# Four attention layers on one core: the third layer's scaling and turning one slot each behind the step before

## What is computed

```python
x = L0(x)   # group norm; q, k, v = h @ w + b (128 wide); softmax(q k / sqrt(C)) @ v + h, over all 256 positions
x = L1(x)   # q, k 16 wide with relu; softmax within a row of 16 positions; gamma * out + x
x = L2(x)   # q, k 16 wide; softmax over all 256 positions; gamma * ctx + x
x = L3(x)   # 8 heads; keys and values from the 3x3 / stride 2 average pool of x; projection w_o, + x

# L2, the third layer, is the one that is changed
q = x @ Wb; k = x @ Wc; v = x @ Wd
attn = softmax(einsum('bnk,bmk->bnm', q, k), axis=-1)
return gamma * einsum('bnm,bmd->bnd', attn, v) + x
```

## Time and profile before

| | before |
|---|---|
| median of the runs | 136.36 us |
| the profiled execution | 136.52 us |
| its span, first to last instruction | 134.6 us |
| granted TensorE clock, mean | 0.975 |
| TensorE busy | 123.1 us (91%) |
| VectorE, ScalarE, GpSimd busy | 83.7, 76.7, 73.2 us |
| third layer, from the first scores to the last output matmul | 55.4 to 80.3 us |

### The profile page before, as it was taken

The page is one execution under the profiler, slowest core; times in us unless marked ns, Lnnn a source line. Parts: engine busy times, 40 slices in busy tenths (PEclk is TensorE's granted clock), DMA queues, the critical chain, the costliest instruction groups (busy, mean ns, idle before and its releaser), DMA issues.

```text
span 134.6 us, 3603 instructions
## 1 busy us (share of the span) xinstructions
PE 123.1 (91%) x1386; PEld 89.6 (67%) x1386; DVE 83.7 (62%) x196; ACT 76.7 (57%) x228; POOL 73.2 (54%) x120
## 2 busy tenths in 40 slices
PE   6887999989999999999899993999949999999990
PEld 4665799977876777667678871423323775988990
DVE  5776666445324564679779430779699999940081
ACT  0436347788985657576987551333425567597320
POOL 8942616999892123320068888504166666799300
PEclk9999999999999999999999999599995999999999
DMA  3950000000000000000000033424455620000046
GB/s 92 328 172 0 0 5 2 2 0 2 0 5 0 5 0 0 5 0 0 0 0 0 27 102 85 140 83 136 63 70 144 83 22 5 5 0 5 5 124 188
DMA packets 19104, 6.41 MB, mean 48 GB/s; under 512 B 9360, under 2 KB 18960, under 8 KB 19088
## 3 DMA queue, kind: packets, MB, share of 16 engines
q1 hardware_dynamic: 17456, 4.93, 15.5%
q10 hardware_dynamic: 1632, 1.27, 3.2%
HBM read 4.61 MB, written 1.57 MB: 46 GB/s over the span
## 4 chain that ended last, share of the span: by engine, by line
PE 73%; DVE 10%; issue 5%; DMA 4%; POOL 3%; ACT 2%; ACTq 0%; DVEq 0%; POOLq 0%
PE bank L749 11%; PE bank L792 9%; PE bank L694 8%; PE bank L771 8%; PE bank L780 5%; PE bank L713 5%; PE bank L733 5%; DMA x_all<-in_x_dram 4%; PE bank L746 3%; PE bank L685 3%; PE bank L809 3%; PE bank L723 2%; PE bank L760 2%; DVE prob L589 2%; DVE negmax L587 2%
## 5 line engine op out<-in xcount | busy, mean ns | idle before, releaser
L416 ACT ACTIVATE prob<-bank,negmax 128x256 f32<-128x256 f32 (+1 forms) x48 | 19.4, 410 | 14.8 <-DVE negmax L549 10.1
L355 POOL TENSOR_TENSOR prob<-prob,inv 128x512 f32<-128x512 f32 x16 | 16.4, 1044 | 16.0 <-DVE inv L599 16.0
L467 ACT ACTIVATE prob<-prob 128x512 f32<-128x512 f32 x16 | 10.1, 630 | 19.9 <-DVE prob L589 19.9
L771 PE MATMUL bank<-kdiag,qT 128*32 128x512 f32 x128 | 17.4, 666 | 2.2 <-issue 2.2
L749 PE MATMUL bank<-probT,v 128*128 128x256 f32 x64 | 17.1, 389 | 0.7 <-issue 0.7
L694 PE MATMUL bank<-packed,xT 128*128 128x128 f32 (+1 forms) x96 | 15.6, 286 | 0.2 <-ACT prob L416 0.2
L577 DVE SCALAR_TENSOR_TENSOR xT<-bank,packed,xT 128x256 f32<-128x256 f32 x16 | 7.7, 482 | 11.7 <-PE bank L749 6.9
L694 PEld LDWEIGHTS bank<-packed,xT 128*128 128x128 f32 x96 | 13.1, 191 | 1.9 <-issue 1.2
L749 PEld LDWEIGHTS bank<-probT,v 128*128 128x128 f32 x64 | 11.1, 190 | 4.1 <-issue 3.1
L792 PEld LDWEIGHTS bank<-probT,vdiag 128*32 128x32 f32 x512 | 11.7, 113 | 3.0 <-issue 3.0
L587 DVE TENSOR_REDUCE negmax<-bank 128x8 f32<-128x512 f32 x16 | 10.6, 663 | 3.6 <-PE bank L771 3.6
(11 more groups left out here) (102 smaller groups left out, 244.5 us busy)
## 6 DMA issues: line engine op xcount, KB each, us to landing
kdiag<-k_rows SPq DMA_DIRECT2D x32, 64.0 KB, 2.5
out_dram<-x_all SPq DMA_DIRECT2D x8, 128.0 KB, 2.0
x_all<-in_x_dram SPq DMA_DIRECT2D x2, 256.0 KB, 4.1
x_all<-in_x_dram ACTq DMA_DIRECT2D x2, 256.0 KB, 5.5
vdiag<-v_rows SPq DMA_DIRECT2D x8, 64.0 KB, 3.2
packed<-in_pack_dram ACTq DMA_DIRECT2D x1, 321.0 KB, 5.8
k_rows<-kT SPq DMA_DIRECT2D x4, 64.0 KB, 2.1
v_rows<-vt SPq DMA_DIRECT2D x4, 64.0 KB, 2.0
```

What stands on the lines that cost most here:

```text
L355: nc.gpsimd.tensor_tensor(p, p, inv[g][:, t, :].unsqueeze(2).broadcast_to([128, HEADS, KEYS]), ALU.mult)\
L416: last = nc.scalar.activation(prob[g][:, t, 0:keys], psum("scores", layer, g)[:, keys * t:keys * t + keys], ACT.Exp, bias=negmax[g][:, t, ...
L467: nc.scalar.activation(prob[g][:, t, :], prob[g][:, t, :], ACT.Exp).then_inc(s_exp3, 1)
L771: last = mm(ps[STRIP * s:STRIP * s + STRIP, :].rearrange("p (c m k) -> p c k m", c=HEADS, m=HKEY), qT[g][:, 0, HTOK * j:HTOK * j + HTOK], ...
```

## The change

The distances of two steps of the third layer become 1 instead of 2: scaling comes one slot behind the scores (and their exponentials), turning one slot behind the scaling. As the distances add up, all later steps start two slots sooner against scores, values and projections, and the list has two slots less.

```diff
-        steps += [("qk", 2, 1), ("v", 2, 1), ("scores", 2, 3), ("scale", 2, 2), ("probT", 2, 2), ("o", 2, 2)]
+        steps += [("qk", 2, 1), ("v", 2, 1), ("scores", 2, 3), ("scale", 2, 1), ("probT", 2, 1), ("o", 2, 2)]
```

## The result

The changed kernel takes 139.74 us (median of three runs, 138.94 to 139.94) against 136.36 us: a ratio of 1.026, with a 95% interval of 1.022 to 1.030. It is slower by 3.4 us. The profiled execution took 138.94 us with a span of 137.0 us, 2.4 us more than before. Executions with a low clock that took over 1.5% longer than the shortest of the same kernel, such as the profiled one of e1 (150.15 us), are left out of every ratio.

A forecast was written before the change was run, and what follows sets the result against it. Bound by the path from ScalarE's first keys copy (kT) through two DMA round trips to the fourth layer's scores. kT +3.8 us, longer idle +0.1: 136.52 + 3.9 = 140.4, median 0.16 lower, 140.3 us; range 138.3 to 142.1.

The forecast's parts named there:

- The ring: Third layer: VectorE's scaling g waits for ScalarE's exponentials g, ahead of maxima g+1; 2.58 us per image against 2.12.
- The two rivals that needed it to be absent: Third layer: shorter pipeline wins, 135.4 us, 6%; TensorE as most-contended engine sets the pace, 136.4 us, 5%.
- The walk: Third layer followed image by image, from maxima 0 at 56.60 to kT at 77.8, 78.2 with the shared resource.
- The bank's tie: Third layer: a pair of scores waits for banks until the previous odd image's exponentials end; +0.32 us for images 2 and 4.
- The shared resource: Third layer: VectorE's scalings 3 to 6 meet GpSimd's pooling inside the ring; 0 to 0.92 us, 0.45 taken.
- From kT to the scores: First keys' copy through two DMA round trips to the fourth layer's first scores: an unchanged 8.12 us.
- The idle time ahead of the scores: TensorE, done with the third layer at 83.6 to 84.0, idles 2.7 to 3 us before the fourth layer's scores.
- The clock: TensorE's 1.2 GHz stretches: one more or less worth up to about 1.5 us; none taken, +0.1 for longer idle.
- the clock falls once more: Rival: another low clock in the third layer or longer behind the keys; +1.5 us, 141.8 us, 12%.

The follow-up runs named there:

- e1: Kernel before with only the scaling's distance cut to 1, turning left at 2: 139.62 us with the slow execution counted, ratio 1.024.
- e9: Kernel before with scaling at distance 1 and turning at 3, so all later steps keep their old slots: 139.29 us, ratio 1.024.
- e2: Kernel before with only the turning's distance cut to 1, scaling left at 2: 137.41 us, ratio 1.010.
- e3: Changed kernel with VectorE alone taking the maxima of image g+1 ahead of the scaling of g: 138.05 us, ratio 1.013 to the kernel before.
- e4: Changed kernel with ScalarE alone copying the first keys (kT) ahead of exponentials 7: 136.39 us, ratio 1.006 to the kernel before.
- e8: e7 plus, on ScalarE, the copy of the first keys ahead of exponentials 7: 134.41 us, ratio 0.990 to the kernel before.
- e7: e1 with VectorE taking the maxima of image g+1 ahead of the scaling of g: 135.02 us, ratio 0.993 to the kernel before.
- e5: Kernel before with the third layer's queries matmul of image 4 done four times, filling TensorE's idle time: 135.76 us, ratio 0.999.

## Why the prediction was right

It said 140.3 us, 138.3 to 142.1; measured 139.74. Point by point:

- **The ring, 2.58 us per image: right.** 2.59 us at the end of the changed kernel, 2.58 to 2.59 in e9. The two rivals that needed it to be absent fell with it.
- **The walk: right to 0.5 us up to kT.** The first maxima started 0.13 us later than before (56.73), which is in all of these: pair 2, 3 at 61.50 (61.4 said), first output 65.10 (64.9), maxima 4 at 68.20 (67.9), maxima 7 at 76.28 (75.8), exponentials 7 at 77.00 (76.5, with the shared resource 76.95), kT at 78.27 (78.2).
- **The bank's tie: right** in place and kind (1.03 us of wait in both the changed kernel and e2). The two steps that it lengthens are 3.01 and 2.98 us (59.62 to 62.63, 65.22 to 68.20), 0.4 over the ring where 0.32 was said. That the turning's distance was a tie of its own once the ring is open was not seen; e3 showed it.
- **The shared resource: half the price, and partly on the other engine.** One scaling inside the ring took 0.92 us (70.27), the others 0.69: 0.23 us and not 0.45. Scaling 7 took 0.92 us too (79.50), outside the ring but ahead of the last turning, where the sum had nothing. The rest of the meetings was paid by GpSimd: three of its second pooling steps (L369) took 0.94 to 0.98 us, and the chain holds none of them. The other 0.2 us of kT's time are the start's 0.13 and roundings.
- **From kT to the scores, 8.12 us "with nothing in it that the change touches": the term that was mis-sized.** From kT's end (78.64) it was 7.24 us, as the key rows landed sooner. (By its row kT ended at 74.78 before, not 74.76, which makes 8.10.) The time from their issue to the next one was 2.51 us before, 1.61 after, 1.63 or 1.64 in e2, e3, e4 and e8, 1.84 in e7, 2.19 in e9 and 2.33 in e5. It varies by 0.9 us between kernels with the same transfer; what decides it was not tested. One profiled execution isn't enough for such a term.
- **The idle time ahead of the scores: wrong, harmless.** 2.7 to 3 us said, 1.21 measured. The keys came 0.8 us sooner than said, and TensorE was through only at 84.67 (83.6 to 84.0 said), as the prediction named kT as late on ScalarE and overlooked the values' copy and scaling 7 behind it on VectorE. e4 found this.
- **The clock: taken at no change, which it wasn't.** The profiled execution of the changed kernel had no low stretch for two before, which is worth the 0.60 us behind the scores. Its other two executions had about one each and took 0.8 and 1.0 us longer. So the rival "the clock falls once more" names something that these kernels do; its price of 1.5 us was somewhat high.
- **The number is nearer than the terms.** The two terms, 0.9 + 0.6 us, are why the profiled execution (138.94) is 1.5 us below the sum of 140.4 for it. The median is only 0.6 us below the forecast because two of the three executions had a low stretch that the profiled one didn't have. That is luck. At the full clock the loss is about 3.0 us: 138.94 for 135.9, the middle of the 27 executions of the kernel before at 0.996 or more that stand beside the experiments (the two were not run side by side).

## What to carry to other kernels

In a list that all engines walk in order, a step's distance is not only latency: it decides which instruction stands behind which wait. Before a distance goes from 2 to 1, add up one turn of the engines that then wait for each other (here 2.58 us against 2.12), and put the instruction that feeds the other engine ahead of the one that waits for it. And look for the one short copy that a DMA chain starts from: moved ahead of work that doesn't need it, it gave 2.7 us here.

## What the runs showed of the hardware that was not expected

- The same 64 KB write from the chip to memory took 1.61 to 2.51 us until its waiting successor was issued, in nine traces. In e5 the program up to the write is that of the kernel before, and its 2.33 us for 2.51 is a spread between executions alone.
- One stretch of some 3.4 us with TensorE at 1.2 GHz cost 0.5 to 1.4 us in e2, e3, e4 and e7, and from nothing to 1.3 us in the kernel before. Inside the bare ring of e9 the step stayed at 2.59 us with the clock at 1.2 GHz.
- TensorE's clock fell at the end of a short wait in the third layer or behind it: 0.70 us in e9, 1.03 us in e2 and e4. It did not fall behind the same wait of 1.03 us in the profiled execution of the changed kernel. What decides that isn't shown.
- When a VectorE operation with two inputs in SBUF and a GpSimd one met, the first to start kept its time: the scaling took 0.92 us when GpSimd's step had begun 0.02 us ahead of it (70.25), and GpSimd's step took 0.98 us when it began 0.02 us behind the scaling (73.10 and 73.08). The Trainium skill (SBUF — State Buffer, Who interferes with whom) says that whoever starts first holds the shared ports; the trace agrees on who pays, and the price was 0.23 us on VectorE's side, less than the 0.38 us that were left of GpSimd's step, and about 0.5 on GpSimd's (0.98 us for 0.44 of the same step alone).
